# Expert stage: one gelu instruction on two banks for VectorE's pairs, and signals by pair

## The chip, the cores and the metric

The kernel runs on one core of a Trainium2 chip. The metric is the time of one execution on the device, in microseconds (us). Five engines work side by side, each in the order of its own program, and meet at semaphores: TensorE (PE, matrix products into PSUM), ScalarE (ACT, functions by element), VectorE (DVE), GpSimd (POOL) and SyncE (SP, which starts DMA transfers). PSUM has eight banks of 512 float32 values in each of 128 partitions; POOL does not read it in this kernel.

## The reference

The program embeds 64 images of 16 patches and 64 texts of 77 words into 64 x 93 = 5952 tokens of 192 values, adds an attention-like layer, and then adds a layer of small experts. That last layer is what the change is about. Cut to it:

```python
# xf: 5952 tokens x 192; S=8 slots, R=16, M=64 experts a slot, K=4 chosen, H=32, G=64
z = jnp.einsum('nd,sdr->nsr', xf, P)
scores = jnp.einsum('nsr,smr->nsm', z, C)
topv, topi = jax.lax.top_k(scores, K)
w = jax.nn.softmax(topv, axis=-1)
h = jax.nn.gelu(jnp.einsum('nsr,nskrh->nskh', z, W1[sidx, topi]) + b1[sidx, topi])
yl = jnp.einsum('nskh,nskhr->nskr', h, W2[sidx, topi]) + b2[sidx, topi]
comb = jnp.einsum('nskr,nsk->nsr', yl, w).reshape(n, S * R)
out = jax.nn.gelu(comb @ G1 + g1b) @ G2 + g2b      # gelu: the tanh form
```

The kernel does not gather. It computes the hidden values of all 8 x 64 experts for every token and multiplies them by a gate that is zero for those that were not chosen.

## The kernel before, in words

Three stages follow each other: embedding, attention with the gates (both of which the change leaves alone), and the expert stage, which goes over 12 tiles of 496 tokens.

**A tile of the expert stage.** 512 experts of 32 hidden units are 128 chunks of 128 rows. Two chunks make a *duo* (64 a tile), two duos a *quad* (32 a tile). For each duo, in this order:

1. PE makes the hidden products, `hidden` (L1642): for each of the two chunks four products of 32 columns, side by side in the four column groups of PE, into one bank of PSUM. The bank holds 128 x 496 values.
2. ACT takes the gelu, `gelu`.
3. The gated product: DVE (`gate_duo`, L1408), one instruction for each bank, reads PSUM and the gates and writes SBUF; or POOL (`gate_duo`, L800), one instruction for the duo, which reads SBUF. `POOL_DUOS` lists 22 duos of a tile for POOL, no two in a row; the other 42, `DVE_DUOS`, are DVE's, and duos 0 to 3 are all among them.
4. PE decodes a quad (`decode`, L1655), which adds its share to the code of the tile in an eighth bank, four quads after the quad's hidden products.

**What sets the order.** It is written out. PE runs hidden products of a quad's two duos, then one `decode`, and so on; after duos 21, 27 and 31 come the three output products of the tile before (`out1`, L1665, and two of `out2`, L1674). ACT takes duos in order, with the copy of the finished code of the tile before after duo 7 (L1032) and the output's gelu after duo 21 (L1036). DVE and POOL take their duos in order.

**The ring.** The first seven banks are a ring. The slots of a tile are the two banks of each duo and one for each output product, in PE's order, so a bank is used again seven slots, three and a half duos, later. PE waits in `bank_free` for whoever read the bank last: the DVE gate of that bank (`s_gat`), ACT for a duo of POOL's (`s_hid`), or the engine that reads an output product. A duo whose first slot is the ring's last bank lies on banks 6 and 0, which do not adjoin; `WRAPS` lists these: 3, 10, 17, 27, 30, 33, 40, 47, 54, 61, of which 40 is POOL's.

**Signals.** `s_hp1` counts banks made by PE, `s_hid` gelus done, `s_gat` and `s_pg` gated products. For a duo of DVE's, ACT waits for each bank, takes its gelu in place, in PSUM (L1016), and signals it; DVE waits for each bank. For a duo of POOL's, ACT waits for both banks, takes both in one instruction into an SBUF buffer of two places (L1028; L1024 twice for duo 40), and signals once. SP counts `s_hp1` to know when the codes of the next tile may be loaded over those of this one.

Of the kernel before, what the change touches and what calls it, by code (L numbers as in the profile page):

```python
# [27 lines left out]
ACT = mybir.ActivationFunctionType  # L28
# [42 lines left out]
DUOS = 2 * QUADS  # L71
POOL_DUOS = [d for d in range(4, DUOS) if d % 11 in (1, 4, 7, 9)]
DVE_DUOS = [d for d in range(DUOS) if d not in POOL_DUOS]
# [24 lines left out]
def wait(eng, sem, value):  # L98

    if isinstance(value, int) and value <= 0:  # L100
        return
    eng.wait_ge(sem, value)


def dve_gated(tile, duo, piece=1):

    before = sum(d < duo for d in DVE_DUOS)
    return 2 * (len(DVE_DUOS) * tile + before) + (1 + piece if duo in DVE_DUOS else 0)


def banks_gelu(tile, duo, piece=1):

    full = len(POOL_DUOS) + 2 * len(DVE_DUOS)
    before = sum(1 if d in POOL_DUOS else 2 for d in range(duo))
    return full * tile + before + (1 + piece if duo in DVE_DUOS else 1)


def pool_gated(tile, duo):

    return len(POOL_DUOS) * tile + sum(d <= duo for d in POOL_DUOS)  # L120


def bank_of(x):

    return SLOT_OF[x] % RING


def bank_user_before(tile, x):

    at = SLOT_OF[x] - RING  # L130
    while True:
        if at < 0:
            at, tile = at + len(SLOTS), tile - 1
        user = SLOTS[at]
        if user and not (isinstance(tile, int) and tile <= 0 and isinstance(user[0], str)):
            return tile, user
        at -= RING


def first_of_quad(duo, mine):  # L140

    return duo % 2 == 0 or duo - 1 not in mine


def parts(duo):

    quad = duo // 2
    block, k = divmod(quad, KH)
    return quad, block, k, 2 * (duo % 2)


def build(nc, t):

    with ExitStack() as ctx:
        def sem(name):
            return ctx.enter_context(nc.semaphore(name))
# [159 lines left out]
        hid = c3(128, [2, 2, TN])  # L316
# [66 lines left out]
        s_hp1, s_hid = sem("hidden_product"), sem("hidden_gelu")  # L383
        s_gat, s_pg = sem("hidden_gated"), sem("hidden_gated_by_pool")
# [4 lines left out]
        def wait_apart(eng, *waits):  # L389


            held = [(sm, v if isinstance(v, int) else eng.to_reg(v)) for sm, v in waits]
            if any(not isinstance(v, int) for _, v in held):
                eng.wait_ge(s_const, 1)
            for sm, v in held:
                wait(eng, sm, v)


        def duo_banks(duo):

            low = bank_of((duo, 0))
            assert duo not in WRAPS
            return ring[:, low:low + 2, 0:TN]

        def duo_bank(duo, k):

            return ring[:, bank_of((duo, k)), 0:TN]
# [6 lines left out]
        def chunk(s, hb, k):  # L414

            return (s * KH + k) * EB + hb
# [12 lines left out]
        def units_first(ap, e):  # L429

            return ap.rearrange("p (e k m h) -> p e k h m", e=EB, k=KH, m=16)[:, e]

        def stacked(ap, e):

            return ap.rearrange("p (k h e m) -> p e k h m", e=EB, k=KH, m=16)[:, e]
# [31 lines left out]
        def _(sp):  # L467
# [105 lines left out]
            def load_codes(tile, half):  # L573
                for i in range(6):
                    sp.dma_start(zst[R * i:R * i + R, half],
                                 zq_r[ZP[i], half, :, :, bass.ds(tile * TN, TN)]).then_inc(s_zl[half], 16)

            def load_gates(tile, o):
                for h in range(2):
                    sp.dma_start(gst[64 * h:64 * h + 64, o],  # L580
                                 gq_r[o, :, :, bass.ds(tile * TN, TN)]).then_inc(s_gl[o], 16)
# [33 lines left out]
            def refill(tile, o):  # L615


                wait_apart(sp, (s_hp1, 2 * DUOS * (tile - 1) + DUOS * (o + 1)))
                load_codes(tile, o)
                last = DUOS // 2 * (o + 1) - 1  # L620
                wait_apart(sp, (s_gat, dve_gated(tile - 1, last)), (s_pg, pool_gated(tile - 1, last)))
                load_gates(tile, o)

            refill(1, 0)
            refill(1, 1)
            for i in range(0, (TILES - 2) // 2):
                for k in range(2):
                    tile = 2 * i + 1 + k
# [14 lines left out]
        def _(pool):  # L643
# [148 lines left out]
            def gate_duo(tile, duo):  # L792

                quad, block, k, j = parts(duo)
                if duo == first_pool[block // EB]:
                    pool.wait_ge(s_gl[block // EB], 32 * (tile + 1))
                if first_of_quad(duo, POOL_DUOS):
                    wait(pool, s_code, QUADS * tile + quad - SPACES + 1)
                pool.wait_ge(s_hid, banks_gelu(tile, duo))
                p_.tensor_tensor(gated[:, quad % SPACES, j:j + 2], hid[:, POOL_DUOS.index(duo) % 2],  # L800
                                 gst[:, block // EB, j:j + 2], ALU.mult).then_inc(s_pg, 1)

# [20 lines left out]
        def _(act):  # L823
            a_ = nc.scalar
# [23 lines left out]
            for jj in range(JJ):  # L848
# [16 lines left out]
                if jj == 8:  # L865
# [3 lines left out]
                    for g in range(EB):  # L869
                        for o in range(2):  # L870
                            last = a_.copy(w2o[:, g, o, :, :, 16 * o:16 * o + 16], w2v[:, g, o])
# [137 lines left out]

            def gelu(tile, duo):  # L1010

                if duo in DVE_DUOS:
                    for k in range(2):
                        act.wait_ge(s_hp1, 2 * (DUOS * tile + duo) + k + 1)
                        product = duo_bank(duo, k)
                        a_.activation(product, product, ACT.Gelu_apprx_tanh).then_inc(s_hid, 1)  # L1016
                    return
                act.wait_ge(s_hp1, 2 * (DUOS * tile + duo + 1))
                to_pool = hid[:, POOL_DUOS.index(duo) % 2]
                wait(act, s_pg, pool_gated(tile, duo) - 2)  # L1020
                if duo in WRAPS:
                    for k in range(2):
                        product = duo_bank(duo, k)
                        last = a_.activation(to_pool[:, k], product, ACT.Gelu_apprx_tanh)  # L1024
                    last.then_inc(s_hid, 1)
                else:
                    product = duo_banks(duo)
                    a_.activation(to_pool, product, ACT.Gelu_apprx_tanh).then_inc(s_hid, 1)  # L1028

            def copy_code(tile):  # L1030
                act.wait_ge(s_code, QUADS * (tile + 1))
# [24 lines left out]
        def _(dve):  # L1056
# [95 lines left out]
            for e in range(EB):  # L1152
                last = v_.tensor_tensor(stacked(w1r, e), units_first(w1f, e), stacked(w1h[:, 0], e), ALU.subtract)
# [246 lines left out]
            def gate_duo(tile, duo):  # L1400
                quad, block, k, j = parts(duo)
                if duo == first_dve[block // EB]:
                    dve.wait_ge(s_gl[block // EB], 32 * (tile + 1))
                if first_of_quad(duo, DVE_DUOS):
                    wait(dve, s_code, QUADS * tile + quad - SPACES + 1)
                for p in range(2):
                    dve.wait_ge(s_hid, banks_gelu(tile, duo, p))
                    v_.tensor_tensor(gated[:, quad % SPACES, j + p], duo_bank(duo, p),  # L1408
                                     gst[:, block // EB, j + p], ALU.mult).then_inc(s_gat, 1)

# [31 lines left out]
        def _(pe):  # L1442
# [174 lines left out]
            def bank_free(tile, x):  # L1617

                before, (user, piece) = bank_user_before(tile, x)
                if user == "f1":  # L1620
                    wait(pe, s_y1, before)
                elif user == "f2_0":
                    wait(pe, s_out, 2 * before - 1)
                elif user == "f2_1":
                    wait(pe, s_out, 2 * before)
                elif user in POOL_DUOS:
                    wait(pe, s_hid, banks_gelu(before, user))
                else:
                    wait(pe, s_gat, dve_gated(before, user, piece))

            def hidden(tile, duo):

                quad, block, k, j = parts(duo)
                o, eb = divmod(block, EB)
                if duo % (DUOS // 2) == 0:
                    pe.wait_ge(s_zl[o], 96 * (tile + 1))
                for p in range(2):
                    bank_free(tile, (duo, p))
                    x = chunk(2 * (j + p) + o, eb, k) * 128
                    bank = duo_bank(duo, p)  # L1640
                    for q in range(4):
                        mm = t_.matmul(bank[32 * q:32 * q + 32], w1s[:, x + 32 * q:x + 32 * q + 32], zst[:, o, j + p],  # L1642
                                       start=True, stop=True)
                    mm.then_inc(s_hp1, 1)

            def decode(tile, quad):

# [116 lines left out]
```

## Time and profile before

| | us |
|---|---|
| median of 2 runs | 1491.0 (1490.36 to 1491.64) |
| the profiled execution's own time | 1490.83 |
| its span, first to last instruction | 1488.9 |
| engines busy over the span: PE, DVE, ACT, POOL | 1279.1, 1162.5, 1083.9, 1057.5 |

Busy time counts an engine from the start of an instruction to its end, and where instructions overlap the union. Instructions that follow each other without a wait overlap in part, so the mean length of one is more than what it costs its engine; the distance between the ends of two such instructions is the cost. The names are those of the program: `ring` is the ring of seven banks, `code` the eighth, `arena` the large SBUF buffer, `w_stack` and `w_pad` the weights of the two expert layers, `g1w` and `g2w` those of the output. PEld is PE's loading of weights, which overlaps its products. A product in 32 columns stands in the trace as one instruction, so a bank of hidden products counts four and a decode eight, and a float32 product counts twice. The expert stage fills the span from about 740 us on.

### The profile page before, as it was taken

How to read it: one execution, taken by the hardware profiler on the slowest of the kernel's cores; microseconds unless marked ns; L12 is line 12 of the kernel's file. 1: busy time of each engine (PE TensorE's matmuls, PEld its weight loads, DVE VectorE, ACT ScalarE, POOL GpSimd, SP SyncE). 2: the span in 40 equal slices, each digit the busy share in tenths (PEclk: the TensorE clock that was granted, in tenths of full speed). 3: DMA queues.
4: the chain of work that ended last, by engine and by line, in shares of the span. 5: the costliest groups of instructions: out<-in, count | busy, mean ns of one | idle time of the engine just before them, and what ended most of it. 6: DMA issues, size and time to landing. Idle time of an engine off the chain costs nothing.

```text
span 1488.9 us, 34181 instructions
## 1 busy us (share of the span) xinstructions
PE 1279.1 (86%) x12216; PEld 650.2 (44%) x12216; DVE 1162.5 (78%) x3407; ACT 1083.9 (73%) x2675; POOL 1057.5 (71%) x771
## 2 busy tenths in 40 slices
PE   4743888889888888886699999999999999999996
PEld 3632555555555665553233333333333333333332
DVE  5671388888888888886688888888888888888884
ACT  1242355556655556553599999999999999999995
POOL 6660367667666666664488888888888888888885
PEclk8865899999999999997599999999999999999998
DMA  9635412221121111223312313223132131322310
GB/s 267 134 97 75 63 33 65 66 81 60 57 66 62 58 57 59 63 72 86 94 40 46 79 45 86 60 47 83 45 82 60 46 84 45 81 60 46 86 40 12
DMA packets 93640, 103.81 MB, mean 70 GB/s; under 512 B 12244, under 2 KB 90604, under 8 KB 93190
## 3 DMA queue, kind: packets, MB, share of 16 engines
q1 hardware_dynamic: 89120, 92.76, 24.3%
q10 hardware_dynamic: 2240, 5.08, 2.4%
q0 software_dynamic: 2112, 3.79, 1.1%
q8 instruction: 98, 1.61, 0.5%
q14 instruction: 70, 0.57, 0.1%
HBM read 64.83 MB, written 33.52 MB: 66 GB/s over the span
## 4 chain that ended last, share of the span: by engine, by line
ACT 32%; PE 28%; DVE 24%; issue 7%; POOL 3%; DMA 3%; SPq 2%; ACTq 1%; POOLq 0%; DVEq 0%
ACT ring L1016 19%; ACT arena L1028 9%; PE ring L1642 7%; PE code L1655 6%; DVE arena L1207 5%; DVE arena L1408 4%; PE ring L1528 4%; DVE arena L1196 3%; PE ring L1498 2%; DVE arena L1216 2%; PE ring L1539 2%; PE ring L1674 2%; DMA arena<-in_x 1%; ACT arena L884 1%; DVE arena L1288 1%
## 5 line engine op out<-in xcount | busy, mean ns | idle before, releaser
L1408 DVE TENSOR_TENSOR arena<-ring,arena 128x496 f32<-128x496 f32 x1008 | 611.5, 667 | 132.6 <-ACT ring L1016 131.4
L800 POOL TENSOR_TENSOR arena<-arena 128x992 f32<-128x992 f32 x264 | 608.5, 2315 | 122.7 <-ACT arena L1028 113.3
L1016 ACT ACTIVATE ring<-ring 128x496 f32<-128x496 f32 x1008 | 549.1, 701 | 10.3 <-PE ring L1642 10.3
L1642 PE MATMUL ring<-arena,w_stack 99*32 99x496 bf16 x6144 | 427.8, 376 | 26.6 <-DVE arena L1408 20.9
L1655 PE MATMUL code<-arena,w_pad 128*32 128x496 f32 x3072 | 389.6, 581 | 3.7 <-ACT arena L1032 3.4
L1642 PEld LDWEIGHTS ring<-arena,w_stack 99*32 99x32 bf16 x6144 | 160.4, 95 | 410.5 <-DVE arena L1408 239.4
L1028 ACT ACTIVATE arena<-ring 128x992 f32<-128x992 f32 x252 | 287.0, 1139 | 0.0
L1498 PE MATMUL ring<-arena 96*128 96x372 f32 x384 | 142.0, 502 | 9.1 <-ACT arena L898 7.7
L1655 PEld LDWEIGHTS code<-arena,w_pad 128*32 128x32 f32 x3072 | 96.5, 110 | 56.5 <-DVE arena L1408 17.9
L733 POOL TENSOR_TENSOR arena<-arena 128x372 f32<-128x372 f32 x96 | 91.7, 975 | 37.1 <-DVE arena L1257 36.8
L1498 PEld LDWEIGHTS ring<-arena 96*128 96x128 f32 x384 | 72.7, 197 | 79.1 <-issue 25.7
L1539 PE MATMUL ring<-arena 128*128 128x376 f32 x192 | 79.1, 524 | 25.2 <-DVE arena L1260 21.6
L727 POOL TENSOR_TENSOR arena<-arena 124x512 f32<-124x512 f32 x48 | 58.7, 1223 | 57.4 <-DVE arena L1226 57.2
L898 ACT ACTIVATE arena<-ring 128x93 f32<-128x93 f32 x384 | 94.7, 303 | 0.0
L898 ACT ACTIVATION_READ_ACCUMULATOR arena<-ring 128x1 f32 x384 | 89.0, 262 | 0.0
L741 POOL TENSOR_TENSOR arena<-arena 128x372 f32<-128x372 f32 x96 | 80.7, 861 | 11.5 <-DVE arena L1275 11.5
L884 ACT ACTIVATE arena<-arena 124x192 f32<-124x192 f32 x96 | 45.6, 539 | 47.9 <-DVE arena L1189 47.5
L1207 DVE MATCH_REPLACE8 arena<-arena 124x72 f32<-124x72 f32 x384 | 78.3, 215 | 0.0
L706 POOL TENSOR_SCALAR arena<-arena 124x3 f32<-124x3 f32 x32 | 7.6, 237 | 94.1 <-DVE arena L1182 94.1
L1558 PE MATMUL code<-arena 128*124 128x192 f32 x384 | 70.2, 334 | 3.9 <-POOL arena L741 3.9
L1257 DVE TENSOR_TENSOR arena<-arena,ring 128x372 f32<-128x372 f32 x96 | 51.0, 532 | 27.2 <-PE ring L1539 26.9
L926 ACT ACTIVATE arena<-arena 128x93 f32<-128x93 f32 x16 | 6.0, 372 | 88.3 <-DVE arena L1296 88.3
(134 smaller groups left out, 1666.8 us busy)
## 6 DMA issues: line engine op xcount, KB each, us to landing
arena<-gates SPq DMA_DIRECT2D x48, 496.0 KB, 6.7
gates<-arena SPq DMA_DIRECT2D x16, 744.0 KB, 10.5
arena<-h_scratch SPq DMA_DIRECT2D x32, 279.0 KB
arena<-z_parts SPq DMA_DIRECT2D x144, 62.0 KB, 2.3
h_scratch<-arena SPq DMA_DIRECT2D x16, 279.0 KB
z_parts<-arena SPq DMA_DIRECT2D x48, 93.0 KB, 1.8
arena<-h_scratch SPq DMA_DIRECT2D x12, 372.0 KB
out_h<-arena SPq DMA_DIRECT2D x12, 372.0 KB
```

The costliest lines, as they stand in the source:

```text
L733: p_.tensor_tensor(w2pi[:, c], wpi[:, c], wv[:, c], ALU.mult).then_inc(s_w2pi, 1)
L741: p_.tensor_tensor(o, o, natt[:, c].unsqueeze(2).to_broadcast([128, UB, N]), ALU.mult).then_inc(s_o, 1)
L800: p_.tensor_tensor(gated[:, quad % SPACES, j:j + 2], hid[:, POOL_DUOS.index(duo) % 2], gst[:, block // EB, j:j + 2], ALU.mult).then_inc(s_ ...
L898: last = a_.activation(wsq[:, c, N * b:N * b + N], src[:, N * b:N * b + N], ACT.Square, accum_out=n2[:, c, b:b + 1])
L1016: a_.activation(product, product, ACT.Gelu_apprx_tanh).then_inc(s_hid, 1)
L1028: a_.activation(to_pool, product, ACT.Gelu_apprx_tanh).then_inc(s_hid, 1)
L1207: last = v_.match_replace(mr[:, s, g], v4[:, s, g], sc[:, s, g], CHOSEN)
L1408: v_.tensor_tensor(gated[:, quad % SPACES, j + p], duo_bank(duo, p), gst[:, block // EB, j + p], ALU.mult).then_inc(s_gat, 1)
L1498: mm = t_.matmul(o, wq[:, h, 128 * c:128 * c + 128], xT["A"][:, h], start=(h == 0), stop=(h == 1))
L1539: t_.matmul(pair0[:, c % 2, 0:UB * (N + 1)], headsel[:, c], pis.rearrange("p b n -> p (b n)"), start=True, stop=True).then_inc(s_pb, 1)
L1642: mm = t_.matmul(bank[32 * q:32 * q + 32], w1s[:, x + 32 * q:x + 32 * q + 32], zst[:, o, j + p], start=True, stop=True)
L1655: mm = t_.matmul(code_bank[32 * j:32 * j + 32, 0:TN], w2p[:, chunk(2 * j + o, eb, k)], gated[:, quad % SPACES, j], start=(quad == 0), stop ...
```

## The change

ACT's `gelu` treats all duos alike: it waits once for both banks, and then works on both in one instruction, in place for DVE's duos and into SBUF for POOL's as before; duos in `WRAPS` get two instructions and one signal, on the second. PE signals a duo once, behind the last product of its second bank. DVE waits once for a duo's gelu and then issues its two gated products, each of which still signals its own bank. `banks_gelu`, which counted signals, goes. SP's count for the refill is halved. The hidden products stand in column groups before and after.

```diff
@@ SP, refill
-                wait_apart(sp, (s_hp1, 2 * DUOS * (tile - 1) + DUOS * (o + 1)))
+                wait_apart(sp, (s_hp1, DUOS * (tile - 1) + DUOS // 2 * (o + 1)))
@@ POOL, gate_duo
-                pool.wait_ge(s_hid, banks_gelu(tile, duo))
+                pool.wait_ge(s_hid, DUOS * tile + duo + 1)
@@ ACT, gelu
-                if duo in DVE_DUOS:
-                    for k in range(2):
-                        act.wait_ge(s_hp1, 2 * (DUOS * tile + duo) + k + 1)
-                        product = duo_bank(duo, k)
-                        a_.activation(product, product, ACT.Gelu_apprx_tanh).then_inc(s_hid, 1)
-                    return
-                act.wait_ge(s_hp1, 2 * (DUOS * tile + duo + 1))
-                to_pool = hid[:, POOL_DUOS.index(duo) % 2]
-                wait(act, s_pg, pool_gated(tile, duo) - 2)
+                act.wait_ge(s_hp1, DUOS * tile + duo + 1)
+                to_pool = hid[:, POOL_DUOS.index(duo) % 2] if duo in POOL_DUOS else None
+                if duo in POOL_DUOS:
+                    wait(act, s_pg, pool_gated(tile, duo) - 2)
                 if duo in WRAPS:
                     for k in range(2):
                         product = duo_bank(duo, k)
-                        last = a_.activation(to_pool[:, k], product, ACT.Gelu_apprx_tanh)
+                        last = a_.activation(product if to_pool is None else to_pool[:, k], product,
+                                             ACT.Gelu_apprx_tanh)
                     last.then_inc(s_hid, 1)
                 else:
                     product = duo_banks(duo)
-                    a_.activation(to_pool, product, ACT.Gelu_apprx_tanh).then_inc(s_hid, 1)
+                    a_.activation(product if to_pool is None else to_pool, product,
+                                  ACT.Gelu_apprx_tanh).then_inc(s_hid, 1)
@@ DVE, gate_duo
+                dve.wait_ge(s_hid, DUOS * tile + duo + 1)
                 for p in range(2):
-                    dve.wait_ge(s_hid, banks_gelu(tile, duo, p))
                     v_.tensor_tensor(gated[:, quad % SPACES, j + p], duo_bank(duo, p),
                                      gst[:, block // EB, j + p], ALU.mult).then_inc(s_gat, 1)
@@ PE, bank_free
-                    wait(pe, s_hid, banks_gelu(before, user))
+                    wait(pe, s_hid, DUOS * before + user + 1)
@@ PE, hidden (inside and behind the loop over the two banks)
-                    mm.then_inc(s_hp1, 1)
+                mm.then_inc(s_hp1, 1)
```

ACT from duo 62 of a tile to duo 8 of the next, before. Each row is a run of like instructions; brackets hold the semaphores that it waits for (`hidden_product` is `s_hp1`, `hidden_gelu` is `s_hid`):

```order
L1028 ACTIVATE arena<-ring 128x992 [waits hidden_gated_by_pool,hidden_product]
L1016 ACTIVATE ring<-ring 128x496 [waits hidden_product] x10
L1028 ACTIVATE arena<-ring 128x992 [waits hidden_gated_by_pool,hidden_product]
L1016 ACTIVATE ring<-ring 128x496 [waits hidden_product] x4
L1028 ACTIVATE arena<-ring 128x992 [waits hidden_gated_by_pool,hidden_product]
L1032 COPY arena<-code 128x496 [waits chunk_decoded]
L1016 ACTIVATE ring<-ring 128x496 [waits hidden_product] x2
```

The same place in the change (line numbers are 10 or 11 lower there):

```order
L1017 ACTIVATE arena<-ring 128x992 [waits hidden_gated_by_pool,hidden_product]
L1017 ACTIVATE ring<-ring 128x2x496 [waits hidden_product] x4
L1012 ACTIVATE ring<-ring 128x496 [waits hidden_product]
L1012 ACTIVATE ring<-ring 128x496
L1017 ACTIVATE arena<-ring 128x992 [waits hidden_gated_by_pool,hidden_product]
L1017 ACTIVATE ring<-ring 128x2x496 [waits hidden_product] x2
L1017 ACTIVATE arena<-ring 128x992 [waits hidden_gated_by_pool,hidden_product]
L1022 COPY arena<-code 128x496 [waits chunk_decoded]
L1017 ACTIVATE ring<-ring 128x2x496 [waits hidden_product]
```

Ten one-bank gelus, each with a wait of its own, are four on two banks with a wait each and two for duo 3, whose second does not wait; no instruction has moved to another place.

DVE around the two output sums of a tile, before (`chunk_decoded` is `s_code`, which frees a place for a quad):

```order
L1408 TENSOR_TENSOR arena<-ring,arena 128x496 [waits hidden_gelu,chunk_decoded]
L1408 TENSOR_TENSOR arena<-ring,arena 128x496 [waits hidden_gelu]
L1419 TENSOR_TENSOR arena<-ring,arena 124x384 [waits out_stored0,h1_loaded,g2_product]
L1408 TENSOR_TENSOR arena<-ring,arena 128x496 [waits hidden_gelu,chunk_decoded]
L1408 TENSOR_TENSOR arena<-ring,arena 128x496 [waits hidden_gelu]
```

And in the change:

```order
L1398 TENSOR_TENSOR arena<-ring,arena 128x496 [waits hidden_gelu,chunk_decoded]
L1398 TENSOR_TENSOR arena<-ring,arena 128x496
L1409 TENSOR_TENSOR arena<-ring,arena 124x384 [waits out_stored0,h1_loaded,g2_product]
L1398 TENSOR_TENSOR arena<-ring,arena 128x496 [waits hidden_gelu,chunk_decoded]
L1398 TENSOR_TENSOR arena<-ring,arena 128x496
```

The second gated product of a duo no longer waits for a gelu; the first waits for the gelu of both banks.

## Rows read from the trace of the kernel before

**Rows 1.** The page: busy tenths in 40 slices of the span.

```profile
ACT  1242355556655556553599999999999999999995
...
PEclk8865899999999999997599999999999999999998
```

**Rows 2.** Stretches of the expert stage: busy us by engine, clock, DMA.

```profile
core 0: us, PE busy (x) PEld busy (x) DVE busy (x) ACT busy (x) POOL busy (x), PEclk, DMA share, GB/s
820.00:880.00 60.00, 57.87 (x761) 21.74 (x763) 50.25 (x84) 59.09 (x107) 50.85 (x23) 1.00 0.29 65
...
sum 600.00, PE 579.03 PEld 218.77 DVE 502.56 ACT 591.23 POOL 502.31; mean PE 57.90 PEld 21.88 DVE 50.26 ACT 59.12 POOL 50.23
```

**Rows 3.** Line of the code copies: min/median/max ns, first and last start.

```profile
L1032 ACT COPY arena<-code x11: 627/631/632, 797.2 to 1415.9; 128x496 f32<-128x496 f32 x11
```

**Rows 4.** Time axis, 983 to 1013: start us, us, engine, [idle before <- releaser].

```profile
988.71 2.42 DVE L1408 TENSOR_TENSOR arena<-ring,arena 128x496 f32<-128x496 f32 x4 [0.39 <-ACT ring L1016]
...
990.60 0.39 PE L1642 MATMUL ring<-arena,w_stack 99*32 99x496 bf16 x4 [0.16 <-DVE arena L1408]
...
1002.82 1.04 ACT L1016 ACTIVATE ring<-ring 128x496 f32<-128x496 f32 x2 [0.31 <-PE ring L1642]
...
1006.79 1.02 PE L1642 MATMUL ring<-arena,w_stack 99*32 99x496 bf16 x16
...
1007.23 2.00 ACT L1016 ACTIVATE ring<-ring 128x496 f32<-128x496 f32 x4 [0.60 <-PE ring L1642]
...
1007.93 2.42 DVE L1408 TENSOR_TENSOR arena<-ring,arena 128x496 f32<-128x496 f32 x4 [0.86 <-ACT ring L1016]
...
1009.11 1.02 ACT L1028 ACTIVATE arena<-ring 128x992 f32<-128x992 f32 x1
...
1010.01 2.02 ACT L1016 ACTIVATE ring<-ring 128x496 f32<-128x496 f32 x4
```

**Rows 5.** By line and shape, 820 to 1420: count, busy us, mean ns, idle.

```profile
L1016 ACT ACTIVATE ring<-ring 128x496 f32<-128x496 f32 x817 | 444.6, 699 | 8.8 <-PE ring L1642 8.8
...
L1028 ACT ACTIVATE arena<-ring 128x992 f32<-128x992 f32 x203 | 230.9, 1137 | 0.0
...
L1024 ACT ACTIVATE arena<-ring 128x496 f32<-128x496 f32 x20 | 11.5, 675 | 0.0
```

**Rows 6.** Waits, 760 to 1440: us in total, times, longest us.

```profile
DVE arena L1408 <- ACT ring L1016: 109.3, 229, 0.9
...
ACT ring L1016 <- PE ring L1642: 9.4, 21, 0.6
...
PE code L1655 <- ACT arena L1032: 3.4, 11, 0.3
```

**Rows 7.** Chain that ended last, 900 to 962: start us, us, what.

```profile
by line: ACT ring L1016 39.0%; ACT arena L1028 18.4%; PE ring L1642 12.8%; PE code L1655 11.4%; DVE arena L1408 7.8%; issue 5.4%; PE ring L1674 2.9%; PE ring L1665 1.6%; ACT arena L1024 1.0%; DVEq L1407 0.1%
...
929.65 2.43 DVE arena L1408 x4
932.12 0.60 PE ring L1642 x8
932.73 0.98 PE ring L1665 x2
933.70 0.97 PE code L1655 x8
934.67 0.84 PE ring L1642 x16
935.51 0.83 PE code L1655 x8
...
938.86 0.88 PE ring L1674 x4
...
943.22 0.92 PE ring L1674 x4
...
949.10 1.06 ACT ring L1016 x2
```

More of the change, by code:

```diff
@@ L108, in dve_gated @@
     return 2 * (len(DVE_DUOS) * tile + before) + (1 + piece if duo in DVE_DUOS else 0)
[L111 to L115, printed above, removed]
 def pool_gated(tile, duo):
```

## The prediction

> **What bounds the kernel now.** I read the page first, then the time axis, then the waits, then the chain. The page [rows 1] shows ScalarE (ACT) at nine tenths or more in every slice of the second half, which is the expert stage, and TensorE's granted clock in its top tenth there apart from the stage's first slices. Cut into stretches of 60 us [rows 2], that stage is the same everywhere: ACT 98% busy, TensorE (PE) 96%, VectorE (DVE) 84%, POOL 84%, and the clock at 1.00, which is the 2.4 GHz level. The copies of the finished code, one a tile, are 11 in 618.7 us [rows 3], so a tile of 64 duos takes 61.87 us; twelve of them are half of the kernel, and nothing outside this stage is touched.
>
> Busy shares of ACT and PE that near to each other don't say which one is the limit, so I work out ACT's own pace. Four one-bank gelus from 1007.23 end at 1009.23, the two-bank one after them ends at 1010.13, the next four at 1012.03 [rows 4]: 0.475 us for a bank, 0.95 us for two of them, 0.90 us for two banks in one instruction. (The means in [rows 5], 699 and 1137 ns, are longer because instructions overlap; the distance between ends is what counts.) A tile has 42 duos that DVE gates and 22 that POOL gates, one of those in two instructions: 43 x 0.95 + 21 x 0.90 = 59.8 us, and the code copy and the output gelu, at a bank's pace each, another 0.95: 60.7 of 61.87. The rest is ACT standing still, and of that the waits name PE for 9.4 us in 11 tiles, about 0.85 a tile [rows 6].
>
> The chain over one tile [rows 7] shows how near the others are: 57% of it is gelu, but once in the tile it goes over to DVE for four gates (2.43 us at 929.65) and then stays on PE for some 17 us, through the three output products. So ACT is the limit with a small reserve behind it, and the reserve is what the change has to be measured against.
>
> **The change, part by part.** *Merged gelus.* A DVE duo whose two banks adjoin gets one instruction. Nine of the 42 start in the ring's last bank and keep two. 33 x (0.95 - 0.90) = 1.6 us of ACT a tile, 18 us in twelve. No row shows a two-bank gelu that writes PSUM; the nearest is the two-bank one into SBUF [rows 4], and one-bank gelus take about as long into either (699 ns into PSUM, 675 into SBUF [rows 5]), so I take 0.90. The other end is 0.95, no gain.
>
> *Signals by pair.* This is the cost. The ring has seven banks, three and a half duos, and a bank comes back to PE only when DVE has read it. I follow one return, from the first product of a quad to PE's first product three quads (six duos) later, when nothing else is in the way. Before: PE's start to the gelu's start 0.44 (1006.79 to 1007.23), a one-bank gelu on an idle ACT 0.57 (the pair at 1002.82 takes 1.04, less 0.475), gelu's end to the gate 0.13 (1007.93), four gates 2.42, on to PE 0.05 (the gates from 988.71 are 0.585 apart and the last of a row takes 0.66, so the third ends at 990.55; PE starts at 990.60) [rows 4]; then PE finishes that duo, two banks at 0.21, and decodes for 0.83 [rows 7]. Sum 4.87 us. ACT needs 4 x 0.95 + 2 x 0.90 = 5.60 us for six such duos. The ring is 0.73 us faster than ACT: that is the reserve, and it is what hides output products, the copy of the code and the start of a tile now.
>
> After: ACT may start only when the second bank is made, +0.21; DVE may start only when both banks have their gelu, 0.57 + (0.90 - 0.475) = 1.00 in place of 0.57, +0.43. The return takes 5.51 us, and ACT's own six duos 6 x 0.90 = 5.43. **The reserve is gone**: ring and ACT are level, so what was hidden now adds up. That DVE starts later costs DVE itself nothing (84% busy, and it waits for ACT 109 us already [rows 6]); what is queued behind its wait is the rest of its gates, and the one who waits for those is PE, which has no bank. The signals that SyncE waits for, the codes' refill by half tiles, come at most one bank (0.21 us) later for a transfer with half a tile of room; I put them at nothing. POOL's duos were signalled by pair already.
>
> The new tile: 64 / 6 returns of 5.51 us = 58.8. Output products on PE 0.98, 0.88 and 0.92, each with a decode behind it that takes 0.97 and not 0.83 [rows 7]: 3.2. The tile's first four duos all go to DVE, so the return there has five gates, not four: +0.58. PE's first decode waits for ACT's copy, 3.4 us in 11 tiles [rows 6]: +0.3. A return that starts at a POOL duo has one more gelu (0.90) in place of a gate (0.58) and one product less (0.21): +0.11, in about one of three, +0.4. Sum 63.2 us against 61.87: +1.35 a tile, **+16 us in twelve**. With the profiled execution's 1490.83 that is 1507; the median of the runs shown is 1491.0, the same to 0.2.
>
> Both ends: if half of the output products stays hidden and POOL's extra too, 63.3 becomes 61.2, and the kernel 1483. If the two-bank gelu into PSUM takes 0.95 and ends 1.04 after its start, ACT's 59.8 + 0.95 and the same additions (3.2 + 0.6) make 64.5, with POOL's 0.4 64.9: +32 to +36, 1523 to 1527.
>
> DVE is at 84% in a stage where ACT is the full engine, and it stands still only until ACT's next gelu [rows 2, 6]. The Trainium skill (Perfetto Trace Analysis, Optimizing Scalar/DVE Operations) says that where these engines aren't saturated but cause bubbles on others, breaking instructions up may let work complete sooner. It speaks against joining the gelus, and in the same direction as my sum; the undivided signal is the part of the change that it bears on. By it the time is that of the sum, 1507; were the bubbles of no account, it would be 1473 (A, below).
>
> **The rivals.** *A. ACT stays the limit and gets faster.* For it: ACT is 98% busy, DVE and POOL have a sixth of their time free, and PE makes ACT wait only 0.85 us a tile [rows 2, 6]. Then the 1.6 us are kept: 60.3 a tile, 1473, faster by 1.2%. It decides if the return stays clearly below ACT's 5.43, say at 4.9; for that DVE and PE would have to run further ahead than the 0.6 us by which my two terms lengthen the return. Against it: that the chain already leaves ACT for DVE and PE for a third of each tile [rows 7] with the reserve there. Chance 0.10. The Trainium skill (same page and section) says that grouping into larger operations can improve throughput if the engine is saturated, and gives ScalarE's overhead on PSUM as about 51 ns an instruction; 396 fewer instructions would be an estimated 20 us by it, 1471. The trace's 0.05 us agrees with the figure.
>
> *B. The two-bank gelu in place brings no shorter service.* Then nothing pays for the longer return: 1523 to 1527, slower by over 2%. Against it: the two-bank gelu to SBUF does gain 0.05, from the same banks. Chance 0.15.
>
> *C. The change isn't what it says.* The nine duos at the ring's seam keep two gelus but get the late signal: for them the return is longer by 0.04 more (0.57 + 0.475 against 1.00), with no gain. That is 0.4 us a tile at most and lies in my range, so it has no chance of its own.
>
> **How the numbers follow.** My forecast, 1483 to 1520 around 1507, has 0.75, A 0.10, B 0.15. The range reaches from 1487, below which lie A and the last tail of my low end, to 1524, where B begins to be cut: about 0.8. A measurement of this kernel is told from no change at about 2%, 1461 and 1521. Faster than that takes more than A gives: 0.02. Slower takes B, or my high end: 0.12 (B is not certain to pass the bound). Within: 0.86.
>
> **What would show it.** 396 two-bank gelus ring to ring with an end-to-end distance of 0.90 (or 0.95: B), and 216 one-bank ones left. ACT busy down from 98% to about 94%, its waits for PE up from 0.85 to some 4 us a tile, at many duos and not just at the output products. Code copies 63.2 us apart. PE standing longer until DVE's gates, DVE longer until the gelus, and a chain that goes from gelu to gate to PE every few duos. A clock that stays at 1.00. I am wrong if ACT's wait for PE stays at about 1 us a tile and the copies come 60 to 61 us apart: then the ring had more reserve than the return shows. If ACT's waits grow less than its service shrinks, it is the sum of hidden terms that I have too high.

## The result, and the profile after

The changed kernel takes 1513.8 us (two runs, 1510.48 and 1517.17) against 1491.0: a ratio of 1.0151, 95% interval [1.0097, 1.0206]. It is slower, by 23 us in the medians; the profiled execution, at 1510.48, stands 19.65 us above the profiled one of before.

Stretches of the expert stage after, as in [rows 2] (the columns are busy us and instructions of PE, PEld, DVE, ACT, POOL, then clock and DMA):

```profile
820.00:880.00 60.00, 57.73 (x750) 20.60 (x746) 49.17 (x82) 57.16 (x72) 48.54 (x23) 1.00 0.30 65
...
sum 600.00, PE 577.00 PEld 207.36 DVE 491.21 ACT 567.43 POOL 488.86; mean PE 57.70 PEld 20.74 DVE 49.12 ACT 56.74 POOL 48.89
```

ACT is busy for 567 of 600 us, 94.6%; before it was 98.5%. Its service is shorter, and still it stands idle 3.3 us in every 60, where that was 0.9. The clock is 1.00 as before, so no part of the difference comes from there.

The line of the code copies, as in [rows 3]:

```profile
L1022 ACT COPY arena<-code x10: 579/580/581, 799.4 to 1371.5; 128x496 f32<-128x496 f32 x10
```

Ten copies are nine tiles, 572.1 us: 63.57 us a tile against 61.87. Twelve tiles at 1.70 us make 20 us, which is about the whole difference of the two profiled executions. This spacing is the measure that I use below, because it leaves out the two stages ahead.

The gelus by shape, as in [rows 5] (count, busy us, mean ns, idle time just before):

```profile
L1017 ACT ACTIVATE ring<-ring 128x992 f32<-128x992 f32 x311 | 302.7, 998 | 30.9 <-PE ring L1632 28.5
L1017 ACT ACTIVATE arena<-ring 128x992 f32<-128x992 f32 x199 | 201.4, 1012 | 0.7
...
L1012 ACT ACTIVATE ring<-ring 128x496 f32<-128x496 f32 x170 | 89.6, 578 | 0.9
```

And the waits, as in [rows 6] (us in total, times, longest):

```profile
DVE arena L1398 <- ACT ring L1017: 97.8, 211, 1.2
...
ACT ring L1017 <- PE ring L1632: 29.6, 42, 1.0
...
DVE arena L1398 <- ACT ring L1012: 25.1, 43, 0.8
```

The two-bank gelu takes 998 ns in the mean in place and 1012 into SBUF, so in place it is the shorter of the two. ACT's waits for PE have grown from 9.4 us to 29.6 in about eleven tiles, and DVE's for ACT from 109 to 123 (97.8 and 25.1).

One return of banks, on the time axis as in [rows 4] (start us, us, engine, line, names, count, idle before it):

```profile
902.93 1.01 PE L1632 MATMUL ring<-arena,w_stack 99*32 99x496 bf16 x16
...
903.58 1.00 ACT L1017 ACTIVATE arena<-ring 128x992 f32<-128x992 f32 x1
...
904.47 1.88 ACT L1017 ACTIVATE ring<-ring 128x992 f32<-128x992 f32 x2
...
905.56 2.42 DVE L1398 TENSOR_TENSOR arena<-ring,arena 128x496 f32<-128x496 f32 x4 [0.48 <-ACT ring L1017]
...
907.46 0.39 PE L1632 MATMUL ring<-arena,w_stack 99*32 99x496 bf16 x4 [0.19 <-DVE arena L1398]
...
907.67 1.01 PE L1645 MATMUL code<-arena,w_pad 128*32 128x496 f32 x8
...
908.51 1.01 PE L1632 MATMUL ring<-arena,w_stack 99*32 99x496 bf16 x16
...
946.88 1.02 PE L1632 MATMUL ring<-arena,w_stack 99*32 99x496 bf16 x16
...
947.52 0.98 ACT L1017 ACTIVATE ring<-ring 128x992 f32<-128x992 f32 x1 [1.02 <-PE ring L1632]
...
948.61 0.67 DVE L1398 TENSOR_TENSOR arena<-ring,arena 128x496 f32<-128x496 f32 x1 [0.28 <-ACT ring L1017]
```

PE starts a quad at 902.93. ACT takes its first duo, one of POOL's, at 903.58, 0.65 us later: 0.21 for the second bank and the 0.44 of [rows 4]. (For POOL's duos ACT waited for both banks in the kernel before too, so in this return the 0.21 is not new.) Two joined gelus follow at 904.47. DVE starts behind the first of them at 905.56; it stood still until then. Four gates in a row; the third ends at 907.40 and PE, which had stopped, has its bank at 907.46, decodes at 907.67 and starts the quad three quads further at 908.51. The return is 5.58 us; for this kind, which begins with a duo of POOL's, the prediction had 5.62. Six duos in 5.58 us are 59.5 us a tile before a single output product is made. Two joined gelus in a row take 1.88 and one on an idle ACT takes 0.98 (947.52), so another one costs 0.90.

The last three rows are the start of a quad whose first duo is DVE's, where both signals come later than before: 0.64 us from PE's first product to the gelu and 1.73 to the gate. Before it was 0.44 and 1.14 (1006.79, 1007.23 and 1007.93 in [rows 4]). The gate comes 0.59 us later; the prediction's two terms add up to 0.64.

The chain over the same stretch, as in [rows 7] (start us, us, what):

```profile
903.10 0.45 PE ring L1632 x8
...
903.58 1.00 ACT arena L1017
904.57 0.90 ACT ring L1017
...
905.56 0.84 DVE arena L1398 x2
...
906.74 0.68 DVE arena L1398
...
907.46 0.39 PE ring L1632 x4
907.85 0.83 PE code L1645 x8
908.68 0.45 PE ring L1632 x8
...
915.76 2.43 DVE arena L1398 x4
```

It goes PE, gelu, gelu, gate, PE and round again in six duos: in this stretch no engine is the limit, the ring is. It is not so all through the tile: from 909.15 to 915.7 the same chain goes from gelu to gelu on ACT.

### The profile page after: what moved, and what is told of

Same layout as the page of the kernel before. It is cut to its first block, busy times and chain, and to the rows that moved or that the text cites. A ratio compares the mean times of both kernels' runs of the same rounds, so it can differ in the third digit from the quotient of the medians.

```text
span 1508.7 us, 33785 instructions
## 1 busy us (share of the span) xinstructions
PE 1296.1 (86%) x12216; PEld 644.6 (43%) x12216; DVE 1166.2 (77%) x3407; ACT 1073.6 (71%) x2279; POOL 1057.1 (70%) x771
## 4 chain that ended last, share of the span: by engine, by line
DVE 30%; PE 29%; ACT 23%; issue 9%; POOL 4%; DMA 3%; SPq 2%; ACTq 1%; DVEq 0%; POOLq 0%
DVE arena L1398 11%; ACT ring L1017 9%; PE ring L1632 7%; PE code L1645 7%; ACT arena L1017 6%; DVE arena L1197 4%; PE ring L1518 4%; DVE arena L1186 3%; DVE arena L1206 2%; ACT ring L1012 2%; PE ring L1488 2%; PE ring L1529 2%; PE ring L1664 2%; DMA arena<-in_x 1%; ACT arena L877 1%
## 5 line engine op out<-in xcount | busy, mean ns | idle before, releaser
L1632 PE MATMUL ring<-arena,w_stack 99*32 99x496 bf16 x6144 | 441.8, 377 | 26.4 <-DVE arena L1398 18.4
L1017 ACT ACTIVATE ring<-ring 128x992 f32<-128x992 f32 x396 | 385.5, 998 | 35.6 <-PE ring L1632 32.6
L1632 PEld LDWEIGHTS ring<-arena,w_stack 99*32 99x32 bf16 x6144 | 155.5, 95 | 439.7 <-DVE arena L1398 293.1
L1017 ACT ACTIVATE arena<-ring 128x992 f32<-128x992 f32 x252 | 255.0, 1012 | 1.4 <-PE ring L1632 0.6
L1012 ACT ACTIVATE ring<-ring 128x496 f32<-128x496 f32 x216 | 113.8, 578 | 1.8 <-PE ring L1632 0.6
L720 POOL TENSOR_TENSOR arena<-arena 124x512 f32<-124x512 f32 x48 | 58.6, 1221 | 59.5 <-DVE arena L1216 59.3
```

What stands on the lines that cost most here:

```text
L1012: last = a_.activation(product if to_pool is None else to_pool[:, k], product, ACT.Gelu_apprx_tanh)
L1017: a_.activation(product if to_pool is None else to_pool, product, ACT.Gelu_apprx_tanh).then_inc(s_hid, 1)
```

## The experiments

Two theories. **R** is the prediction's: a pair's signals lengthen the way of a bank back to PE, and the seven banks don't cover it. **J**: the joined gelu itself costs, for instance because it holds two banks of PSUM that others want; the signals are harmless. Spacing is a tile's, from the copies' rows that follow; ratios, with 95% intervals, are against runs of the kernel before on the same chip at the same time (medians 1492.5 to 1494.5 us; 1491.0 for the change).

| kernel | ratio | tile, us |
|---|---|---|
| before | 1 | 61.87 |
| the change | 1.0151 [1.0097, 1.0206] | 63.57 |
| PE's signal by pair alone | 1.0048 [1.0028, 1.0067] | 62.48 |
| DVE's wait by pair alone | 1.0134 [1.0102, 1.0166] | 63.50 |
| both, gelus not joined | 1.0221 [1.0186, 1.0256] | 64.53 |
| 18 duos joined | 0.9926 [0.9900, 0.9952] | 61.15 |
| the other 15 joined | 1.0131 [1.0097, 1.0166] | 63.57 |
| six banks, before | 1.0172 [1.0121, 1.0223] | 63.98 |
| six banks, the change | 1.0614 [1.0564, 1.0664] | 69.31 |
| half gates, before | 0.9966 [0.9944, 0.9988] | 61.29 |
| half gates, the change | 0.9927 [0.9903, 0.9951] | 60.82 |

### The signals without the joined gelus

Edit to the changed kernel, so that DVE's duos take two gelus and one signal:

```diff
-                if duo in WRAPS:
+                if duo in WRAPS or duo in DVE_DUOS:
```

> The change without its joined gelus: PE signals a duo, ACT takes its two banks one after the other (0.95 us), DVE waits for both. Theory R (the return of a bank is longer than the ring allows): the return is longer by 0.21 and 0.475 us and nothing is gained, so it must be slower than the change: 1515 to 1527 us, ACT's idle time 2.5 us a tile or more. Rival J (the joined gelu itself costs, because it holds two banks of PSUM): the signals are harmless, 1488 to 1496.

```profile
L1022 ACT COPY arena<-code x10: 590/592/594, 805.1 to 1385.9; 128x496 f32<-128x496 f32 x10
```

(1385.9 - 805.1) / 9 = 64.53 us a tile: 2.66 more than before and 0.96 more than the change. The median, 1527.0, is at the upper end of R's 1515 to 1527 and far above J's 1488 to 1496. So the signals cost, and the joined gelus give a part back. (That part rests on the spacing of the tiles: the intervals of the two ratios overlap slightly, 1.0186 to 1.0256 against 1.0097 to 1.0206.) J falls with this run.

### One signal at a time

PE's alone, an edit to the kernel before (ACT then waits once for both banks, and SP's count is halved):

```diff
                 for p in range(2):
...
-                    mm.then_inc(s_hp1, 1)
+                mm.then_inc(s_hp1, 1)
```

> The kernel before with only PE's signal by duo; gelus and DVE's waits stay by bank. R: the return is 0.21 us longer out of a reserve of 0.73, so most is hidden: 1491 to 1498. J: no change, 1491.

```profile
L1032 ACT COPY arena<-code x10: 654/658/662, 804.2 to 1366.5; 128x496 f32<-128x496 f32 x10
```

DVE's alone:

```diff
+                dve.wait_ge(s_hid, banks_gelu(tile, duo, 1))
                 for p in range(2):
-                    dve.wait_ge(s_hid, banks_gelu(tile, duo, p))
```

> The kernel before with only DVE's wait by duo: it starts a duo when both one-bank gelus are done, 0.475 us later. R: 0.475 of the reserve of 0.73 goes, and what the reserve hid comes out in part: 1497 to 1510. J: no change, 1491.

```profile
L1032 ACT COPY arena<-code x10: 627/629/634, 802.5 to 1374.0; 128x496 f32<-128x496 f32 x10
```

62.48 and 63.50 us: 0.61 and 1.63 us a tile, 7 and 20 us of the kernel. The later wait of DVE is by far the dearer one. Both came out above what R had expected: 1501.2 in the median against 1491 to 1498, and 1514.6 against 1497 to 1510. So the reserve of 0.73 us does not hide at every return what R let it hide. In both traces the loss arises in the first twenty quads of a tile; the last twelve are at most 0.05 us longer than before. Together the two signals cost 2.66, more than 0.61 + 1.63 = 2.24, which fits two delays that draw on one reserve.

### A shorter ring

Both kernels with `RING = 6`; the seventh bank stays unused. This moves the seam of the ring too: seven of DVE's duos and five of POOL's have banks that don't adjoin, in place of nine and one.

```diff
-RING = 7
+RING = 6
```

> The kernel before with a ring of six banks in place of seven (three duos; the rest of the order as it was). R: PE's restart after a quad now comes back four duos later, over two gates: 0.44 + 0.57 + 0.13 + 1.25 + 0.05 + 0.21 + 0.83 = 3.5 us against ACT's 3.7 for four duos, so the reserve falls from 0.73 to some 0.2 and a part of what it hid comes out: a tile of 62.5 to 64.5 us, 1498 to 1522. J says nothing on it.

```profile
L1032 ACT COPY arena<-code x10: 593/593/593, 800.5 to 1376.3; 128x496 f32<-128x496 f32 x10
```

> The changed kernel with a ring of six banks. R: the same return is 0.64 us longer, 4.1 us, against ACT's 3.6 for four joined gelus, so the ring sets the pace: 16 x 4.1 and the 3.2 us of output products, 68 to 71 us a tile, 1565 to 1600. J (the joined gelu costs by itself): the same 20 us above the kernel before with six banks as with seven.

```profile
L1022 ACT COPY arena<-code x9: 577/579/579, 805.3 to 1359.8; 128x496 f32<-128x496 f32 x9
```

One bank less costs the kernel before 2.11 us a tile and the change 5.74 (69.31 - 63.57). With six banks the change is 5.33 us a tile behind, three times the 1.70 that it is with seven: a fixed cost of the gelu instruction would not grow when a bank is taken away. (A cost of holding two banks could; against that form of J stands the kernel with the signals alone.) Both medians, 1517.6 and 1580.4, lie where R put them.

### A shorter gate

Both kernels with DVE's gates on the first 248 of 496 columns from tile 1 on, so half of the gated products of DVE's duos stay stale:

```diff
+                    w = TN if tile == 0 else TN // 2
-                    v_.tensor_tensor(gated[:, quad % SPACES, j + p], duo_bank(duo, p),
-                                     gst[:, block // EB, j + p], ALU.mult).then_inc(s_gat, 1)
+                    v_.tensor_tensor(gated[:, quad % SPACES, j + p, 0:w], duo_bank(duo, p)[:, 0:w],
+                                     gst[:, block // EB, j + p, 0:w], ALU.mult).then_inc(s_gat, 1)
```

> The kernel before, with DVE gating only the first 248 of 496 columns of its banks in tiles 1 to 11 (the other columns keep what tile 0 or an earlier quad left; the output is not the reference's). R: four gates are some 1.0 us shorter, the reserve grows to 1.7, and ACT alone is left: 60.7 to 61.5 us a tile, 1478 to 1488. J: the same.

```profile
L1032 ACT COPY arena<-code x11: 628/851/854, 793.9 to 1406.8; 128x496 f32<-128x496 f32 x11
```

> The changed kernel with the same half gates (the output is not the reference's). R: the return falls from 5.5 to 4.5 us against 5.3 of six joined gelus (0.889 each), so ACT is the limit again and keeps what the joining saves: 59.3 to 60.7 us a tile, 1460 to 1478, faster than the kernel before with half gates by 8 to 20 us. J: slower than that one by the 20 us that the change costs.

```profile
L1022 ACT COPY arena<-code x11: 612/615/617, 805.5 to 1413.7; 128x496 f32<-128x496 f32 x11
```

61.29 and 60.82 us: with a shorter return the change is the faster one by 0.47 us a tile, its sign turned as R said, but its size is under the expected, 6 us in the medians and not 8 to 20, and its spacing a little over the 59.3 to 60.7. Nor is it shown that ACT alone is left, as R had it for the kernel before with half gates: from 900 to 964 us its chain is for two thirds on PE (32.0% and 31.6% at L1643 and L1656). The shares of the chain in the changed one with half gates, 900 to 964 us:

```profile
by line: ACT ring L1017 29.1%; ACT arena L1017 22.6%; PE code L1646 12.4%; PE ring L1633 12.0%; ACT ring L1012 9.4%; issue 7.5%; PE ring L1665 2.6%; PE ring L1656 1.5%; DVE arena L1399 1.3%; ACT arena L1012 1.1%; ACT arena L1022 1.0%; DVEq 
```

DVE (L1399) has left the chain, 1.3%; but PE has 28% of it. Pieces of the chain around the output products (start us, us, what):

```profile
935.06 0.83 PE code L1646 x6
935.89 0.97 PE ring L1633 x14
...
938.53 0.98 PE ring L1656 x2
...
944.68 0.84 PE ring L1665 x4
...
949.01 0.84 PE ring L1665 x4
949.85 0.97 PE code L1646 x8
952.18 1.04 ACT ring L1012 x2
```

From 935 to 951 the chain stays on PE, through eight decodes and three output products; PE's own work sets the pace there, and ACT's saving finds nothing to shorten. By the first products of the quads, the nine behind the first output product are 0.26 us longer in the change than in the kernel before, both with half gates, and the last twelve of the tile 0.68 us shorter. That PE is all that keeps the missing part was not tried by itself.

### Joining only where the bank isn't waited for

The kernel before, with signals by bank, and joined gelus for 18 of the 33 duos whose banks adjoin. I chose them by following the schedule with the trace's durations: a duo is left alone where its bank is one that PE would wait for. That leaves out duos 0 to 2 in the row of four at the tile's start, eight more duos that start a quad, and four that don't; but eight of the 18 start a quad as well. A joined duo has both late signals with it: ACT waits for its two banks, and DVE's two gates for the one gelu (`banks_gelu` counts it once).

```diff
+JOINED = [5, 6, 8, 11, 13, 19, 25, 36, 38, 39, 41, 44, 46, 49, 50, 52, 55, 57]
...
+                if duo in JOINED:
+                    act.wait_ge(s_hp1, 2 * (DUOS * tile + duo + 1))
+                    product = duo_banks(duo)
+                    a_.activation(product, product, ACT.Gelu_apprx_tanh).then_inc(s_hid, 1)
+                    return
                 if duo in DVE_DUOS:
```

> The kernel before with joined gelus and signals by pair for 18 of DVE's duos (5, 6, 8, 11, 13, 19, 25, 36, 38, 39, 41, 44, 46, 49, 50, 52, 55, 57), picked by following the schedule with the trace's durations so that PE does not wait for their banks; all others stay by bank. R: the 18 gain 0.06 us each (0.95 against the 0.889 measured in the change), 1.1 us a tile, 13 in all, and lose nothing: 1475 to 1486. J: each joined gelu costs its share of the change's 20 us, 11 of it: about 1502.

```profile
L1039 ACT COPY arena<-code x11: 580/580/582, 802.9 to 1414.4; 128x496 f32<-128x496 f32 x11
```

(1414.4 - 802.9) / 10 = 61.15 us, and a ratio of 0.9926 [0.9900, 0.9952]: 10 us faster than the kernel before in the medians, 0.7 us a tile of the 18 x 0.06 = 1.1 that the joining saves on ACT. It lies in R's range of 1475 to 1486, and it is the fastest of the complete kernels here.

The complement, with the other fifteen in that list:

> The other fifteen duos joined (0, 1, 2, 14, 16, 21, 22, 24, 28, 32, 35, 43, 58, 60, 63) and the 18 left by bank. R: these stand at the starts of quads or in the row of four at the tile's start, where PE is waiting for their banks; they save 15 x 0.06 us of ACT but lengthen most of the returns that count: 62.8 to 63.7 us a tile, 11 to 22 us slower than the kernel before. If only the number of joined gelus counted (N), it would be as joined18, some 8 us faster than before.

```profile
L1039 ACT COPY arena<-code x10: 591/595/597, 802.7 to 1374.8; 128x496 f32<-128x496 f32 x10
```

ACT's waits for PE, 760 to 1440 us (us in total, times, longest), first in the kernel with 18, then in the one with 15:

```profile
ACT ring L1023 <- PE ring L1649: 9.9, 22, 0.5
```

```profile
ACT ring L1017 <- PE ring L1649: 31.0, 42, 1.0
```

63.57 us a tile, as expected by R, as slow as the change with all 33, and with about the same waits of ACT for PE, 31.0 us against 29.6; with the eighteen they stay at 9.9, where the kernel before has 9.4. Fifteen duos alone lose as much as the whole change, and the other eighteen alone gain. How many gelus are joined doesn't decide; which ones does. That it goes by the banks PE waits for is how the two sets were chosen, and both results fit it. The change also signals the nine duos at the ring's seam late, which neither of these kernels does; one with all 33 joined and those nine by bank was not run, so how the change's 1.70 us divide among the fifteen, the eighteen and the nine is not shown.

## Why the prediction was right

**The limit before: right.** ACT with a small reserve behind it. That the reserve is one of ring banks and not of ACT was the point on which the forecast hung, and six banks in place of seven showed it (before: +2.11 us a tile).

**Merged gelus: right, a little better than taken.** The prediction took 0.90 for the nearest row, [rows 4]; it costs 0.89 to 0.90 in place, and 0.98 on an idle ACT where 1.00 was taken. Rival B, the price of 0.95, fell here. But of the service saved only a part reached the tile: 0.96 us between the change and the kernel with its signals alone, where 33 x 0.05 to 0.06 are 1.7 to 2.0. That the rest lies in stretches that ACT does not set is likely and not shown. (33 x 0.05 in twelve tiles is 19.8 us and not the prediction's 18, so rival A should have stood at 1471; no other number hangs on it.)

**Signals by pair: right in mechanism and nearly in size.** The two terms of +0.21 and +0.43 are there, +0.59 in all at 946.88, and the return of 5.58 us is near the 5.62 that the sum had for its kind. The sum gave 63.2 us a tile and 1507; the tile is 63.57, and 1510.5 the profiled execution that goes with it. Where in the tile the 1.70 us arise, PE's rows tell: the start of quad 11, which follows the first output product and its decode, of quad 20, and of the next tile's first quad. Before:

```profile
934.49 1.02 PE L1642 MATMUL ring<-arena,w_stack 99*32 99x496 bf16 x16
...
951.79 1.01 PE L1642 MATMUL ring<-arena,w_stack 99*32 99x496 bf16 x16
...
974.83 0.81 PE L1642 MATMUL ring<-arena,w_stack 99*32 99x496 bf16 x12 [0.58 <-DVE arena L1408]
```

And after:

```profile
940.34 1.02 PE L1632 MATMUL ring<-arena,w_stack 99*32 99x496 bf16 x16
...
959.04 1.01 PE L1632 MATMUL ring<-arena,w_stack 99*32 99x496 bf16 x16
...
981.88 0.81 PE L1632 MATMUL ring<-arena,w_stack 99*32 99x496 bf16 x12 [0.55 <-DVE arena L1398]
```

| quads of a tile | before, us | after, us | by the prediction's terms, us |
|---|---|---|---|
| 0 to 10 (what is left of the tile) | 21.53 | 22.03 | 22.3 |
| 11 to 19, with two output products | 17.30 | 18.70 | 18.7 |
| 20 to 31 | 23.04 | 22.84 | 22.2 |

The last twelve quads, where no output product is in the way, lose nothing. Of the 1.70 us, 1.40 arise in the nine quads behind the first output product and 0.50 at the tile's start: what the reserve had hidden comes out there, as the prediction had it. The last column is an estimate of how its terms fall on the three parts (returns of 5.51 us for each three quads, and each addition where it belongs). By it the 0.35 us too little is in the plain returns of the last twelve quads, 0.6 short, less 0.3 too much at the start. So the mechanism was right, and that the total came this near is partly luck: two errors of opposite sign.

**Rival A** (ACT stays the limit, 1473) fell because the return, 5.58 us, is not below the 5.4 that ACT needs for six duos. Its mechanism is real: with half gates the change is the faster one, and with 18 joined duos the kernel before gets faster. The rule of the Trainium skill on grouping (Perfetto Trace Analysis, Optimizing Scalar/DVE Operations) names a saturated engine as its condition, and 98% busy looked like it. The rule of the Trainium skill on breaking instructions up, in the same section, is for engines that aren't saturated but cause bubbles on others. The measurement decides: joining fifteen of the 33 duos, late signals and all, lost 1.70 us a tile, joining the other eighteen gained 0.72.

**The signs.** 396 and 216 gelus, ACT at 94.6% (94 forecast), the clock, DVE's longer waits and the round of the chain came as written. Two did not. ACT's waits for PE are 29.6 us in 680, 2.8 a tile and not 4; a gelu that finds ACT idle takes 0.98 us and not 0.89, and the difference counts as busy, but four of them a tile explain only 0.4 us of it. And there are 42, four a tile, where the prediction had them at many duos and not just at the output products: most of their time lies around the output products, as in the 1.02 us before 947.52, and the rest chiefly at the tile's start. Nor do the shares of the chain rank the causes: in the kernel with DVE's late wait alone they read

```profile
by line: ACT ring L1016 49.1%; ACT arena L1028 23.9%; DVE arena L1408 8.1%; issue 7.4%; PE code L1655 4.3%; PE ring L1642 2.6%; PE ring L1665 1.5%; PE ring L1674 1.4%; ACT arena L1024 0.9%; DVE arena L1419 0.7%; ACT arena L1032 0.2%; DVEq L
```

with DVE at 8.1% where it was 7.8% before [rows 7], though that tile is 1.63 us longer for nothing but DVE's wait. A likely reason is that several ways round are nearly as long and the chain shows one of them.

## What to carry to other kernels

In this kernel it paid to relieve an engine at 98% only where the buffers in front of it came back no later for it. Follow one buffer round before joining instructions or signals: the time of its return against the time in which the busiest engine uses up the ring; if they are within the delay that the joining adds, join only those whose buffer nobody is waiting for. Look first at the stretches in which another engine already has no pause, here PE's through the output products: there the reserve is spent. One kernel with the signals alone and one with a shorter ring tell the two effects apart.

## What the runs showed that was not expected

The gelu on two banks is no dearer in place than into SBUF, but cheaper: 0.98 us on an idle ACT in place (the row at 947.52) and 1.00 into SBUF (903.58). The Trainium skill (ScalarE: Activation LUTs, in the note within Step-by-step: what each stage is for) calls PSUM the faster destination of ScalarE; the trace agrees, by 0.02 us in these two rows.

The same kernel's time spreads more between executions than within the expert stage. Seventeen runs of the kernel before, beside the experiments with six banks and half gates, lay between 1485.1 and 1498.1 us, and the first code copy comes between 793.9 and 805.5 us in the traces above, after two stages that are alike in all of them and one tile, while the tiles of one trace differ by 0.4 us at most. That fits the change's 23 us in the medians of two runs against 20 us by its tiles.
